# Turned activations kept for the query side, and one bias operation in another slot

## The reference

```python
def attn(x):                      # H = 16 heads of 16, F = 64 features
    q, k, v = heads(x, Wq, bq), heads(x, Wk, bk), heads(x, Wv, bv)
    qp, kp = relu(q @ rw) + EPS, relu(k @ rw) + EPS
    kv = einsum('bhsf,bhsd->bhfd', kp, v)
    qkv = einsum('bhsf,bhfd->bhsd', qp, kv)
    norm = einsum('bhsf,bhf->bhs', qp, kp.sum(axis=2))
    return (qkv / (norm[..., None] + EPS)) @ Wo + bo
def ffn(h):
    # scores of 4 heads x 64 x 64 key pairs, top 8, softmax -> idx, w
    w = silu(h . down_embed[idx]) * softmax(scores)
    return silu(h @ Wg + bg) * (h @ Wu + bu) @ Wd + bd + w . up_embed[idx]
x = layernorm(x + attn(x))
x = layernorm(x + ffn(x))
```

## Time and profile before

| | us |
|---|---|
| median of three runs | 3481.85 |
| lowest and highest | 3479.89, 3484.04 |
| profiled execution, its own time | 3480.97 |
| its span in the profile | 3479.1 |
| TensorE busy | 3362.4 (97%) |
| VectorE busy | 2870.6 (83%) |
| ScalarE busy | 1991.4 (57%) |
| GpSimd busy | 1301.9 (37%) |

### The profile page before, as it was taken

How to read it: one execution, slowest core, us unless ns; L and a number is a source line. 1 busy time by engine, 2 the same in 40 slices (tenths; PEclk the granted TensorE clock), 3 DMA queues, 4 the chain that set the end, 5 groups by cost and what they waited for, 6 DMA issues and landing times.

```text
span 3479.1 us, 48605 instructions
## 1 busy us (share of the span) xinstructions
PE 3362.4 (97%) x17888; PEld 2641.6 (76%) x17888; DVE 2870.6 (83%) x5316; ACT 1991.4 (57%) x2886; POOL 1301.9 (37%) x788
## 2 busy tenths in 40 slices
PE   8779999999999999999999999999999999999988
PEld 6457877777777777877777877777877777777767
DVE  4688878988888888888888887888888888888873
ACT  4456556555556555566556566556556565555541
POOL 0234333334333434343334343344333344434441
PEclk9889999999999999999999999999999999999999
DMA  4000000100001000000001000100000000000000
GB/s 122 25 19 31 19 19 31 31 25 31 19 19 31 31 25 31 19 19 31 31 25 31 19 19 31 31 25 31 19 19 31 31 19 25 25 19 25 13 19 19
DMA packets 36762, 94.35 MB, mean 27 GB/s; under 512 B 6832, under 2 KB 11184, under 8 KB 36528
## 3 DMA queue, kind: packets, MB, share of 16 engines
q1 hardware_dynamic: 36528, 91.25, 8.2%
HBM read 57.68 MB, written 33.55 MB: 26 GB/s over the span
## 4 chain that ended last, share of the span: by engine, by line
PE 82%; DVE 7%; ACT 6%; issue 3%; POOL 2%; DMA 0%; SPq 0%; POOLq 0%; ACTq 0%; DVEq 0%
PE ring L672 26%; PE y_bank L757 11%; PE y_bank L759 11%; PE step_bank L574 6%; PE step_bank L566 5%; PE step_bank L672 4%; PE step_bank L610 3%; PE step_bank L602 3%; PE step_bank L701 3%; PE step_bank L691 3%; PE step_bank L745 3%; DVE prob L1160 2%; PE step_bank L560 2%; POOL grid L479 1%; ACT prob L911 1%
## 5 line engine op out<-in xcount | busy, mean ns | idle before, releaser
L479 POOL TENSOR_TENSOR grid<-ex 128x1024 f32<-128x1024 f32 x512 | 994.5, 1950 | 1469.6 <-ACT ex L892 726.5
L757 PE MATMUL y_bank<-wd_sb,gate 128*128 128x256 f32 x2048 | 622.8, 386 | 9.2 <-DVE wexp L1182 9.2
L759 PE MATMUL y_bank<-up_sb,wexp 128*128 128x256 f32 x2048 | 613.3, 381 | 0.0
L1160 DVE SCALAR_TENSOR_TENSOR prob<-grid,narrow,prob 128x1024 f32<-128x1024 f32 x256 | 580.2, 2266 | 9.0
L672 PE MATMUL ring<-x1T_hl,downT_hl 128*128 128x512 f32 x1536 | 421.2, 410 | 23.8 <-ACT gate L917 23.7
L672 PE MATMUL ring<-x1T_hl,wg_hl 128*128 128x512 f32 x1536 | 430.1, 415 | 5.0 <-DVE gate L1176 5.0
L759 PEld LDWEIGHTS y_bank<-up_sb,wexp 128*128 128x128 f32 x2048 | 391.8, 191 | 54.2
L1147 DVE SCALAR_TENSOR_TENSOR grid<-grid,best 128x1024 f32<-128x1024 f32 x256 | 343.6, 1342 | 107.0 <-POOL grid L479 105.1
L672 PE MATMUL ring<-x1T_hl,wu_hl 128*128 128x512 f32 x1536 | 421.2, 409 | 0.0
L757 PEld LDWEIGHTS y_bank<-wd_sb,gate 128*128 128x128 f32 x2048 | 362.0, 192 | 70.8 <-issue 37.9
L672 PEld LDWEIGHTS ring<-x1T_hl,wu_hl 128*128 128x128 f32 x1536 | 281.9, 188 | 119.6 <-issue 42.9
(11 more groups left out here) (168 smaller groups left out, 5551.2 us busy)
## 6 DMA issues: line engine op xcount, KB each, us to landing
xb<-in_L_attn_x SPq DMA_DIRECT2D x34, 512.0 KB, 4.2
x_kept<-x SPq DMA_DIRECT2D x32, 512.0 KB, 5.1
prob<-x_kept SPq DMA_DIRECT2D x32, 512.0 KB, 3.6
out_y<-x SPq DMA_DIRECT2D x32, 512.0 KB, 2.7
xa<-in_L_attn_x SPq DMA_DIRECT2D x30, 512.0 KB, 3.5
prob<-in_L_ffn_down_embed SPq DMA_DIRECT2D x1, 1024.0 KB, 6.2
prob<-in_L_ffn_Wg SPq DMA_DIRECT2D x1, 1024.0 KB, 10.0
prob<-in_L_ffn_Wu SPq DMA_DIRECT2D x1, 1024.0 KB, 10.7
```

The costliest lines, as they stand in the source:

```text
L479: pool.tensor_tensor(grid[:, h % 2], bcast(ex[:, h, 0:NX].unsqueeze(2), [P, NX, NK]), bcast(ex[:, RH + h, 0:NK].unsqueeze(1), [P, NX, NK]) ...
L757: pe.matmul(rows, gate[:, c % 2, t * P:(t + 1) * P], wd_sb[:, c, :], start=(c == 0 and t % 2 == 0), stop=False, skip_group_check=True)
L759: mm = pe.matmul(rows, wexp[:, c % 2, t * P:(t + 1) * P], up_sb[:, c, :], start=False, stop=(c == C - 1), skip_group_check=True)
L1160: ins = dve.scalar_tensor_tensor(out=row, in0=g, scalar=rz[:, h:h + 1], in1=row, op0=ALU.mult, op1=ALU.add, accum_out=mass[:, 0:1] if h == ...
```

## The change

Three things are different.

The turned rows of a group are written once and used twice. When the two key-side turns of a group have been copied to xaT, SyncE stores xaT (512 KB) in a new array in device memory, xT_kept. For the query side of that group SyncE loads it to xbT, when num(1) of the group before has read qp, in slot 5. The two turns of `AT_SEQ` and ScalarE's two copies are gone, q waits for the load, and before ScalarE writes xaT again it waits until the store has read it. xb is still loaded, for the sum with the attention's output.

GpSimd's bias of xb no longer waits for the turns of xb, only for xb's load.

The residual's bias is one operation of 128x2x512 elements in place of two of 128x512 on [P, 2, D], and stands in slot 4 ahead of that slot's spreads (L524), no longer behind slot 5's.

```diff
-    AT_SEQ = ([[("turn", 0)], [("turn", 1)], [("q", 0)], [("q", 1)]] + [[("qp", j)] for j in range(4)] + [[]]
+    AT_SEQ = ([[], [], [("q", 0)], [("q", 1)]] + [[("qp", j)] for j in range(4)] + [[]]
...
+        xT_kept = nc.dram_tensor("xT_kept", [NG, P, KD, G], F32).ap()
...
+            def keep_turned(a):
+                sp.wait_ge(*drained("kv", a, "turn", 0))
+                sp.wait_ge(*drained("kv", a, "turn", 1))
+                sp.dma_start(xT_kept[a], in_lane(a)[0].xT[:]).then_inc(in_lane(a)[0].kept, 16)
...
+            for k in range(2):
+                keep_turned(2 * FILL - 2 + k)
+            sp.wait_ge(*full("kv", 2 * FILL - 1, "v", 1))
+            sp.wait_ge(xbT_kept, FILL * 16)
+            sp.wait_ge(xaT_kept, 16)
+            sp.dma_start(xbT, xT_kept[0]).then_inc(xbT_loaded, 16)
...
                     sp.dma_start(xa[:], x_groups[a + 1]).then_inc(xa_loaded, 16)
+                if kv:
+                    keep_turned(a)
...
+                if at and m + 1 < NG:
+                    lane, i = in_lane(m + 1)
+                    sp.wait_ge(*full("at", m, "num", 1))
+                    sp.wait_ge(lane.kept, (i + 1) * 16)
+                    sp.dma_start(xbT, xT_kept[m + 1]).then_inc(xbT_loaded, 16)
...
                     pool.wait_ge(xb_loaded, (m + 1) * 16)
-                    pool.wait_ge(*full("at", m, "turn", 1))
...
+                    if ff and c == C // 2:
+                        pool.wait_ge(res_loaded, (n + 1) * 16)
+                        rows = residual(par).rearrange("p i (t d) -> p i t d", t=2)
+                        pool.tensor_tensor(rows, rows, bcast(bd_sb[:].unsqueeze(1).unsqueeze(1), [P, 2, 2, D]),
+                                           ALU.add).then_inc(res_bias, 1)
                     if rt and not odd:
                         spread(t, 0)
                     kv_adds(KV_LATE[c])
                     if rt and not odd:
                         spread(t, 1)
-                    if ff and c == 5:
-                        pool.wait_ge(res_loaded, (n + 1) * 16)
-                        rows = residual(par).rearrange("p i (t d) -> p i t d", t=2)
-                        for i in range(2):
-                            pool.tensor_tensor(rows[:, i], rows[:, i], bcast(bd_sb[:].unsqueeze(1), [P, 2, D]),
-                                               ALU.add).then_inc(res_bias, 1)
...
-                    if kind == "turn":
-                        if j == 0:
-                            pe.wait_ge(xb_loaded, (m + 1) * 16)
-                        mm = turn(at_bank, xb, j)
-                    elif kind == "q":
-                        pe.wait_ge(*drained("at", m, "turn", 1))
+                    if kind == "q":
+                        pe.wait_ge(xbT_loaded, (m + 1) * 16)
                         mm = project(at_bank, wq_sb, xbT, j)
...
+                        act.wait_ge(lane.kept, i * 16)
                     read_by(act.activation(lane.xT[:, j, :], bank[:], ACT.Identity,
...
-                    if kind == "turn":
-                        read_by(act.copy(xbT[:, j, :], at_bank[:]), "at", m, kind, j)
-                    elif kind == "q":
+                    if kind == "q":
...
-                    dve.wait_ge(res_bias, (f + 1) * 2)
+                    dve.wait_ge(res_bias, f + 1)
```

More of the change, by code:

```diff
@@ L161, in block_kernel @@
         xa2_loaded = sem("xa2_loaded")
+        xaT_kept, xbT_kept, xbT_loaded = sem("xaT_kept"), sem("xbT_kept"), sem("xbT_loaded")
         k2_high = sem("k2_high")
```

9 lines of the change are left out of this document (5 added, 4 removed).

## The result

The changed kernel takes 3498.35 us in the median of five runs (3492.97 to 3499.98), the one before 3479.89 in the same comparison (3476.09 to 3484.04). The ratio is 1.0047, with a 95% interval of 1.0034 to 1.0061: slower by half a per cent, above the range of the prediction. The profiled execution is the shortest of the five, 3492.97 us with a span of 3491.2, so the trace explains 12 of the median's 18 us; the rest lies in executions without a trace.

The account below looks back on a forecast made before the run. TensorE, never idle in steady iterations, was held by a GpSimd, VectorE and ScalarE chain. Ordinary +12.4, edges -6.5, ends -5.5, iterations 4 to 6 -3.7 sum to -3.3 us: 3478.5 from 3481.85; range 3460 to 3491, 82%.

Parts of the forecast that it names:

- What TensorE loses of work, and where it can be held: TensorE saves 1.09 us an iteration in slot 0, 34.9 in all; waits at kp(2) and num(1) limit the gain.
- the 2.75 that the forecast gave as a sign: Slot 0 without transposes: TensorE's time from gate to routing would be 2.75 us, against 3.39 before.
- two waits named: TensorE's waits for VectorE before kp(2) in slot 4, slack 0.25 us, and for ScalarE's kp reading before num(1), slack 1.24.
- Slot 4: The residual's single bias on GpSimd in slot 4 delays VectorE's keep (L1147) by 1.49 us.
- +0.30 of the bounds: Bound for an ordinary iteration: +0.30 us if slot 4's delay exists alone.
- The ordinary iteration: Chain 1.85 us later, num(1) starts 0.65 later; 19 iterations at 0.65 give +12.4 us.
- The third rival: GpSimd keeps the port across back-to-back operations in slot 4: kp(2) 2.52 us later, about 3516 us; 9%.
- The earlier xb bias: Bias no longer waiting for transposes delays slot 0's keep by 0.30 us and the chain up to slot 4 by 0.36.
- At a batch's edge ... the gain goes through that, since everything there starts from q(0): At six batch edges TensorE's full saving passes through ScalarE's qp wait: 6 x -1.09 = -6.5 us.
- In the tail TensorE waits for VectorE, so 4 x -1.09 is passed on: Tail: TensorE's saving gives -4.4 us, the residual's bias leaving slot 5 -1.1 over five iterations; sum -5.5.
- The start: Iterations 4 to 6: -2.4 us in iteration 5 and -1.3 for 4 and 6, sum -3.7.
- the fourth rival: Kept rows' load comes late or the change doesn't do what it says: some 3482 to 3486 us; 3%.

Follow-up runs that it names:

- work put back: Changed kernel without its early xb bias and residual change, each half of xa turned twice in every iteration, restoring the number of transposes; 3475.69 us, ratio 0.999.
- kept rows alone: Changed kernel with the residual's bias back as two operations in slot 5 and xb's bias held until slot 0's transposes of prob are full; 3470.83 us, ratio 0.9969.
- run with the early xb bias: Changed kernel with the residual's bias back in slot 5 as two operations, xb's bias still early; 3484.65 us, ratio 1.001.
- kernel before shifted: Kernel before, with each half of xa turned twice in iterations 6, 10, 14, ... 30, none at a batch's edge; 3491.72 us, ratio 1.0032.

## Why the prediction was wrong, step by step

**What TensorE loses of work, and where it can be held: right in the main.** 1.01 of 1.09 us shows in slot 0. The first pair of transposes was worth 0.46, not 0.65: from the gate's start to the scores' it is 2.94 us after, not the 2.75 that the forecast gave as a sign. The work put back shows what this gain is worth in an ordinary iteration, 0.03. Of the two waits named, kp(2) bounds the kept rows alone and num(1) the kernels with the bias in slot 4; that about half of the gain ends earlier, at ScalarE's reading of qp in slot 2, was not seen.

**Slot 4: right in mechanism and size.** 1.54 for 1.49, and +0.33 alone for the +0.30 of the bounds. The ordinary iteration came to +0.72 for +0.65. The third rival (GpSimd keeps the port across two operations) didn't come true: in both places the waiting add went first.

**The earlier xb bias: right in size, by luck.** The chain is 0.40 later behind the second norm, 0.36 was forecast. But the 0.36 was worked out from GpSimd's first spread, which comes sooner and was to hold up more of the four norm operations, with their start left where it was. They start 0.38 later, since the 0.38 at the keep of slot 0 (0.30 forecast, but not counted at the norm) goes on through a VectorE that has no idle time in between, and they take 2.98 for 2.97. In the kept rows alone, with xb's bias held, the spread comes 0.85 sooner behind the mark than before, and the norm ends 0.02 later:

```profile
1480.79 1.90 POOL L504 TENSOR_TENSOR grid<-ex 128x1024 f32<-128x1024 f32 x1 [2.07 <-ACT ex L912]
1480.83 2.98 DVE L1224 TENSOR_SCALAR x<-x,mv,rstd 128x256 f32<-128x256 f32 x4
```

**"At a batch's edge ... the gain goes through that, since everything there starts from q(0)": the step that failed first.** 6 x -1.09 should have been 6 x -0.2, by the edges at full clock of the run with the early xb bias (6 x -0.56 without it). I took TensorE's wait for ScalarE's qp, which follows q(0), for the only one, and passed over q(0)'s own bank, whose reader is VectorE's L1123 at the end of the very chain that I had just made 0.36 later. Slack 0.72 stood in the trace; less 0.36, and 0.05 from a release to a start, it leaves q(0) 0.31 earlier, and 0.30 was measured. That is 5.3 of the miss of 15.3 us in the traced execution.

**The clock: not in the forecast at all.** The profile's page shows a clock of 0.989 in the mean, and of the body one low stretch (iteration 8). I put nothing for it. Five more low edges at 1.1 to 1.35, less 0.3 since the low one of iteration 8 costs less after than the 1.67 that it cost before, make 6 of the 15.3, and with q(0)'s bank the whole miss at the edges (11.3). Neither a rival nor a bound stood for it. Of the median's 18 us another 6 lie in executions without a trace, and what makes them is not known.

**"In the tail TensorE waits for VectorE, so 4 x -1.09 is passed on": a contradiction in itself.** If TensorE waits for VectorE, its saving is lost there. VectorE's rows in iterations 33 and 34 after (beside the earlier trace rows):

```profile
3087.98 3.40 DVE L1162 SCALAR_TENSOR_TENSOR grid<-grid,best 128x1024 f32<-128x1024 f32 x1
...
3111.25 1.27 DVE L1162 SCALAR_TENSOR_TENSOR grid<-grid,best 128x1024 f32<-128x1024 f32 x1
3112.55 1.28 DVE L1175 SCALAR_TENSOR_TENSOR prob<-grid,narrow,prob 128x1024 f32<-128x1024 f32 x1
...
3135.42 2.20 DVE L1162 SCALAR_TENSOR_TENSOR grid<-grid,best 128x1024 f32<-128x1024 f32 x1
```

Slot 4 costs 2.12 (3.40 for 1.28), slot 5 gives back 1.93, the xb bias costs 0.93 at the keep of slot 0, and 0.69 come back behind it where xb's bias used to stand: +0.43, and +0.42 to +0.49 is what each of the four iterations shows. What follows them gives 1.2 back. Forecast -5.5, measured +0.6: 6.1 of the miss.

**The start: -7.0 for -3.7.** Iteration 5 gave 2.3 (forecast 2.4). Iteration 4 gave 4.1: a wait of 1.11 at 99.52 for k(1)'s bank went, and the wo products of 121.26 ran in 1.97 us where before they took 3.58 at a lower clock. The clock again, this time to the good. That is 3.3 in the change's favour, and the ordinary iterations took 1.3 more than forecast.

**The kept rows came in time.** Nothing waits for their load, which lands 3.3 us after issue in the median (40 us ahead of need); the fourth rival has no part in this.

## What to carry to other kernels

An engine at 97% can be bound by a chain that only touches it now and then: before taking work from it, find the latest slack behind work that doesn't start from it. Here 0.9 us of TensorE's work was worth 0.03, and 1.0 us of it 0.60 once VectorE's second norm stood elsewhere (-0.65 with the kept rows, -0.05 without). Where a GpSimd operation holds up a VectorE operation on the chain, its place is worth more than its length, and two pieces are better than one there (+0.18 for +0.33); at the end of slot 5 neither mattered. And when TensorE's clock has low stretches at places that recur, price one more of them at each such place.

## What the runs showed of the hardware

The granted clock fell to 0.50 for q(0) at a batch's edge in none to six of six edges, at 1.1 to 1.7 us each, and which ones depended on when the edges came: the kernel before, with the work at its edges untouched, had it at two more of them with 0.7 us more in one iteration of each batch. It wasn't the idle time ahead (0.45 us at full clock in the run with the early xb bias, none at a low edge of the kernel before shifted) and not the amount of work alone (three of six with eight more transposes). What in the timing decides stays open.

A VectorE operation of two SBUF operands and a GpSimd operation held each other off for their whole lengths in each of the places read, and with both asked for within 0.05 us GpSimd went first by these rows of after (the add took 3.03 for 1.28), and also over a VectorE operation with one tensor operand (L1219, 2.98 us for 1.4).

```profile
1523.90 3.03 DVE L1175 SCALAR_TENSOR_TENSOR prob<-grid,narrow,prob 128x1024 f32<-128x1024 f32 x1
...
1523.95 1.91 POOL L500 TENSOR_TENSOR grid<-ex 128x1024 f32<-128x1024 f32 x1 [3.13 <-DVE prob L1172]
```
The Trainium skill (SBUF — State Buffer, Who interferes with whom) says that whoever issues first gets the ports for the whole instruction; the whole length agrees (3.03 us is the add's 1.28 and most of the spread's 1.91), the order by start doesn't show in these records. It also says that tensor_scalar can contend when it runs in a 2-port mode; L1219 was held up, but in which mode it ran no trace here shows.
